# The next block's normed tokens: computed from the raw ones, turned by VectorE and HBM instead of TensorE

## The reference

```python
def rmsnorm(x, w, eps=EPS):
    return x * jax.lax.rsqrt(jnp.mean(x * x, axis=-1, keepdims=True) + eps) * w

def linear_attention(x, Wq, Wk, Wv, Wo, out_norm_w):
    # q, k, v = x @ Wq, x @ Wk, x @ Wv in 8 heads of 128, in chunks of 128 tokens
    def step(S, qkv):
        qb, kb, vb = qkv
        attn = jnp.einsum('bhid,bhjd->bhij', qb, kb)
        attn = jnp.where(causal, attn, 0.0)
        o = jnp.einsum('bhij,bhjv->bhiv', attn, vb) + jnp.einsum('bhid,bhdv->bhiv', qb, S)
        S = S + jnp.einsum('bhid,bhiv->bhdv', kb, vb)
        return (S, o)
    ...
    return rmsnorm(o, out_norm_w) @ Wo

xn = _layernorm(x, axis=-1)
h = rmsnorm(xn, attn_norm_w)
x1 = xn + linear_attention(h, Wq, Wk, Wv, Wo, attn_out_norm_w)
h = rmsnorm(x1, mlp_norm_w)
s = x1 + jax.nn.silu(h @ Wgate) * (h @ Wup) @ Wdown
g = _silu(ffn_fp4(xn, w_gate, w_up, w_down))
out = x + s * g
```

## Time and profile before

| | us |
|---|---|
| median of 3 runs | 1061.51 |
| lowest, highest | 1060.58, 1062.41 |
| the profiled execution | 1064.03 |
| its span | 1062.3 |

### The profile page before, as it was taken

The page is one execution under the profiler, slowest core; times in us unless marked ns, Lnnn a source line. Parts: engine busy times, 40 slices in busy tenths (PEclk is TensorE's granted clock), DMA queues, the critical chain, the costliest instruction groups (busy, mean ns, idle before and its releaser), DMA issues.

```text
span 1062.3 us, 18981 instructions
## 1 busy us (share of the span) xinstructions
PE 1051.6 (99%) x6790; PEld 960.8 (90%) x6790; DVE 891.8 (84%) x1860; ACT 558.5 (53%) x1604; POOL 47.3 (4%) x68
## 2 busy tenths in 40 slices
PE   9999999999999999999999999999999999999998
PEld 6899999989989999998999889999999999999997
DVE  6788888888877888888777898888888888888887
ACT  6765765756656657657565634443333333333332
POOL 1000000000000000000000000101001010101010
PEclk9999999999999999999999999999999999999999
DMA  6555355455363553654445622253323233323213
GB/s 218 163 171 168 109 173 169 137 157 167 135 191 115 173 179 120 188 171 128 162 149 185 175 73 91 81 159 100 115 90 120 85 120 99 120 85 96 83 59 112
DMA packets 166222, 143.10 MB, mean 135 GB/s; under 512 B 28784, under 2 KB 162928, under 8 KB 166128
## 3 DMA queue, kind: packets, MB, share of 16 engines
q1 hardware_dynamic: 165440, 141.88, 42.9%
q10 hardware_dynamic: 688, 0.00, 0.0%
HBM read 77.27 MB, written 64.57 MB: 134 GB/s over the span
## 4 chain that ended last, share of the span: by engine, by line
PE 88%; DMA 5%; DVE 3%; ACT 2%; SPq 1%; issue 1%; POOL 0%; DVEq 0%; ACTq 0%; POOLq 0%
PE ps L263 69%; PE ps L724 4%; PE ps L776 4%; PE ps L770 4%; PE ps L754 4%; DMA moved<-work 2%; DMA r_gate<-moved 2%; SPq L417 1%; PE ps L859 1%; PE ps L652 1%; PE ps L612 0%; DVE work L1404 0%; DVE work L1521 0%; ACT work L947 0%; ACT work L994 0%
## 5 line engine op out<-in xcount | busy, mean ns | idle before, releaser
L263 PE MATMUL ps<-r_k,r_gate_up 128*128 128x512 f32 x768 | 185.2, 391 | 0.7 <-DVE r_k L1587 0.7
L263 PEld LDWEIGHTS ps<-r_k,r_gate_up 128*128 128x128 f32 x768 | 141.5, 188 | 28.1 <-issue 0.9
L263 PE MATMUL ps<-r_o,onT 128*128 128x256 f32 x768 | 106.8, 288 | 0.0
L263 PE MATMUL ps<-r_h,r_k 128*128 128x512 f32 (+1 forms) x393 | 105.2, 403 | 0.0
L263 PEld LDWEIGHTS ps<-r_q,r_v 128*128 128x128 f32 x768 | 99.7, 191 | 4.9 <-DVE r_v L1655 0.3
L263 PE MATMUL ps<-r_q,r_v 128*128 128x256 f32 x768 | 102.3, 283 | 0.0
L967 ACT ACTIVATE work<-ps 128x128 f32<-128x128 f32 x256 | 67.3, 278 | 59.4 <-PE ps L776 59.1
L263 PE MATMUL ps<-r_h,r_q 128*128 128x512 f32 x384 | 98.2, 391 | 0.0
L263 PE MATMUL ps<-r_v,r_h 128*128 128x512 f32 x384 | 97.4, 390 | 0.0
L263 PEld LDWEIGHTS ps<-r_o,onT 128*128 128x128 f32 x768 | 95.8, 190 | 0.1
L1162 ACT ACTIVATE r_v<-work 128x512 fp32r<-128x512 f32 x64 | 40.5, 633 | 99.2 <-DVE work L1651 99.1
(11 more groups left out here) (161 smaller groups left out, 2054.2 us busy)
## 6 DMA issues: line engine op xcount, KB each, us to landing
moved<-work SPq DMA_DIRECT2D x63, 512.0 KB, 2.9
r_gate<-moved SPq DMA_DIRECT2D x252, 128.0 KB, 2.5
kept_h<-work SPq DMA_DIRECT2D x31, 384.0 KB, 2.6
work<-kept_h SPq DMA_DIRECT2D x124, 96.0 KB, 2.2
work<-in_L_attn_hidden_states SPq DMA_DIRECT2D x15, 512.0 KB, 5.3
kept<-work SPq DMA_DIRECT2D x9, 514.0 KB, 4.4
kept_h<-work SPq DMA_DIRECT2D x9, 512.0 KB, 3.4
kept_xq<-work SPq DMA_DIRECT2D x8, 512.0 KB, 5.6
```

What stands on the lines that cost most here:

```text
L263: done = pe.matmul(out_ap, a, b, start=first and n == 0, stop=last and n == 2, skip_group_check=skip)
```

## The change

`turn_h` leaves TensorE's program. `normed_h` no longer reads `xn` but `x_in`: VectorE makes two factors (`h_factors`, step h = 1), the product of the layer norm's and the rms factor and minus the mean times it, and ScalarE's `normed_h`, now at the end of step h = 1, applies them as scale and bias into `h_sb`. In step h = 2, after `normalize`, VectorE transposes `h_sb` in 32x32 blocks into `x_in`, which nobody needs any more. In step h = 3 SP stores `x_in` to a new HBM tensor `kept_h`, right behind the store of k and o, and loads it back into `h_flat` with its quarters in place, behind the loads of k and o. In step h = 4 ScalarE's `turned_hi` (after `copy_q` and `first_state`) and VectorE's `turned_lo` (first of the early extras, in eight pieces of 128 columns) make `hT`. TensorE's values of that step and their wait go to the step's end, behind the output projection, and ScalarE's copy of them to the end of its step. The piece's transpose into `h_flat` waits for `turned_lo`, `normed_h2` for the store of `x_in`.

```diff
+    kept_h = nc.dram_tensor("kept_h", (HALVES, QUADS, P, KD * CH * QUAD), F32).ap()
...
# SP, exchange (next_h = n + 1 in step h = CH - 1)
                     sp.dma_start(moved.rearrange("b p x -> p b x"), leaving.rearrange("p b i x -> p b (i x)"))\
                       .then_inc(moved_out, 16)
+                    if next_h is not None:
+                        sp.wait_ge(h_turned, KD + next_h)
+                        sp.dma_start(kept_h[next_h % HALVES].rearrange("a p x -> p a x"),
+                                     in_quads(x_in.rearrange("p c d -> p (c d)"))).then_inc(h_stored, 16)
...
+                    if next_h is not None:
+                        sp.wait_ge(h_stored, 16 * next_h)
+                        load_turned(h_flat, kept_h[next_h % HALVES], h_loaded)
...
# TensorE, score_and_project
-                    if h == CH and ahead:
-                        pe.wait_ge(hT_ready, (n0 + s) * KD + 2 * KD)
...
-                    if ahead or h < CH:
+                    if (ahead or h < CH) and h != CH:
                         values(*((1, h, s) if h < CH else (0, h - CH, 1 - s)))
# TensorE, attend
-                    if h == CH - 1 and ahead:
-                        pe.wait_ge(h_ready, n0 + s + 1)
-                        pe.wait_ge(k_perm_ready, t0 + j + 2)
-                        pe.wait_ge(k_ready, t0 + j + 2)
-                        turn_h(0)
-                        pe.wait_ge(attn_ready, t0 + j + 1)
-                        turn_h(1)
...
+                    if h == CH and ahead:
+                        pe.wait_ge(hT_ready, (n0 + s) * KD + 2 * KD)
+                        values(0, 0, 1 - s)
# ScalarE
+                def normed_h(n):
+
+                    act.wait_ge(h_factor_ready, n)
+                    act.wait_ge(gu_ready, n + 1)
                     for c in range(CH):
-                        done = act.activation(h_sb[:, c, :], xn[:, parity, c, :], ACT.Copy, scale=small[:, HR, c:c + 1])
+                        done = act.activation(h_sb[:, c, :], x_in[:, c, :], ACT.Identity, bias=small[:, HB, c:c + 1],
+                                              scale=small[:, HG, c:c + 1])
...
+                def turned_hi(parity, n):
+                    act.wait_ge(h_loaded, 16 * QUADS * n)
+                    for k in range(KD):
+                        act.activation(as_tokens(hT[:, parity, HI, k, :]), landed(h_flat, k), ACT.Copy,
+                                       scale=nw_attn[:, k:k + 1]).then_inc(hT_hi, 1)
...
-                        act.wait_ge(xn_ready, min(value + 1, BLOCKS))
+                        act.wait_ge(h_stored, 16 * min(value, BLOCKS - 1))
...
-                    if h == CH - 1 and ahead:
-                        turned_hi(0, 1 - s, (n0 + s) * KD + KD + 1)
-                        turned_hi(1, 1 - s, (n0 + s) * KD + KD + 2)
+                    if h == CH and ahead:
+                        turned_hi(1 - s, n0 + s + 1)
...
+                    if h == CH and ahead:
+                        copy_v(t0 + j + CH + 1, 0, 0)
...
-                    if h == 2 and ahead:
-                        normed_h(1 - s, n0 + s + 2)
+                    if h == 1 and ahead:
+                        normed_h(n0 + s + 1)
# VectorE
+                def h_factors(parity, mine):
+
+                    settled(dve.tensor_tensor(small[:, HG, :], small[:, HR, :], ln_factor[:, parity, 0, :], ALU.mult), mine)
+                    dve.scalar_tensor_tensor(small[:, HB, :], mv[:, parity, :, 0], -1.0, small[:, HG, :],
+                                             ALU.mult, ALU.mult).then_inc(h_factor_ready, 1)
...
+                def turned_lo(parity, n):
+                    for k in range(KD):
+                        dve.wait_ge(hT_hi, n * KD + k + 1)
+                        for c in range(CH):
+                            done = dve.scalar_tensor_tensor(as_tokens(hT[:, parity, LO, k, :])[:, c],
+                                                            landed(h_flat, k)[:, c], nw_attn[:, k:k + 1],
+                                                            as_tokens(hT[:, parity, HI, k, :])[:, c].bitcast(F32),
+                                                            ALU.mult, ALU.subtract)
+                        done.then_inc(hT_ready, 1)
# early_extras
+                    if h == CH and ahead:
+                        turned_lo(1 - s, n + 1)
                     if h == CH and rounds_piece:
+                        dve.wait_ge(hT_ready, (n + 2) * KD)
                         dve.transpose(h_flat[:, 0:PIECE4[n - 1]].rearrange("p (b t) -> p b t", t=QUAD),
# late_extras
                     if h == 2 and ahead:
                         normalize(1 - s)
-                    if h == CH - 1 and ahead:
-                        turned_lo(0, 1 - s, n * KD + KD + 1)
-                        turned_lo(1, 1 - s, n * KD + KD + 2)
+                        dve.wait_ge(xn_ready, n + 2)
+                        dve.wait_ge(h_ready, n + 1)
+                        turn_blocks(x_in.rearrange("p c d -> p (c d)"), h_flat, h_turned)
# attention, after rms_factor in h == 1
+                        h_factors(1 - s, mine)
```

## The result

The changed kernel takes 1114.87 us (median of 4, 1113.4 to 1115.33) against 1061.12 for the kernel before (median of 4): a ratio of 1.050, with an interval of 1.0486 to 1.0512. The forecast was slower, 1091.5, in a range to 1110; the time lies above it. Its profiled execution took 1114.95 us, span 1113.2.

What follows compares the result with a forecast made beforehand. The prediction took TensorE, busy 99% at full clock, to bound the kernel. Its terms, -6.1 + 2.0 + 0.2 + 3.1 + 31.8 - 0.9, made +30.1: 1094.1 us profiled, 1091.5 in the median, range 1076 to 1110.

Steps and rivals of the forecast that it cites:

- What bounds it, and the sign: Attention part: TensorE bounds the kernel; after the change its fifth steps wait for VectorE's additions; slower, chance 0.92.
- Transposes, -6.1: Fourth steps: removing TensorE's eight transposes saves 0.88 us in each of seven, all on the path, -6.1 us.
- Second step, +2.0: Second steps: two 4-element VectorE operations ahead of turned k cost 0.28 us each, +2.0 us in all.
- Third step, +0.2: Third steps: the earlier normed_h delays k's copy and exchange, but TensorE has values and q meanwhile, +0.2 us in all.
- Fourth step, 3.1 given back of 6.1: Fourth steps: VectorE's block transposes make additions late, losing 0.7 us in four odd blocks, about 0.1 in three even, +3.1.
- Fifth step, +31.8: Fifth steps: TensorE waits for additions behind VectorE's turned_lo, itself waiting for ScalarE; +31.8 us over seven blocks.
- 10.9 + 1.48 + 1.37: Fifth step: additions end at 10.9, then 1.48 to the next scores and 1.37 for values: 13.75 us against 8.92.
- TensorE's clock falls in the gap: Rival: the fifth step's idle gap brings half clock, 3 us lost each; 1101, or 1112 in all blocks; chance 0.18.
- Queues: SP's added store and four loads: the tile lands 0.9 to 1.4 us before ScalarE needs it in the fifth step; no cost.
- the tile lands late: Rival: the tile lands 1.5 us after ScalarE is ready in every block's fifth step, +10, 1101; chance 0.12.
- covered after all: Rival: in the fifth step TensorE does not wait for VectorE's additions; only small terms stay, 1056.7 to 1059.8; chance 0.06.
- HI halves come early: Rival: without VectorE's wait for ScalarE, fifth steps cost only 2.4 us each, 17 in place of 31.8, 1076.7; chance 0.12.

Runs made afterwards that it cites:

- e3: Kernel before with each of the eight TensorE transposes in the fourth step done twice; 1070.15 us against 1062.46, ratio 1.0075.
- e4: Kernel before with only h_factors and the early normed_h (scale and bias, from x_in) added, transposes still on TensorE; 1065.34 us against 1062.46, ratio 1.003.
- e5: e4 plus VectorE's two block transposes at the end of the third step, result unread; 1065.33 us against 1061.62 for the kernel before, ratio 1.0036.
- e2: Changed kernel with the fifth step's turned_lo and piece transpose moved behind VectorE's state additions, weights4_hi behind ScalarE's normed o; 1073.41 us, ratio 1.0113 to the kernel before.
- e1: Changed kernel with 20 extra, later overwritten products filling TensorE's gap in each fifth step; 1100.12 us, ratio 1.0358 to the kernel before.
- e6: e2 with h_factors moved to the second step's late extras and ScalarE's last copy of values ahead of weights4_hi; 1072.09 us, ratio 1.0093 to the kernel before.
- e8: Changed kernel with 10 extra products instead of the 20 of e1 in each fifth step's gap; 1109.56 us, ratio 1.044 to the kernel before.

## Why the prediction was wrong

**What bounds it, and the sign:** right. A VectorE addition behind an early extra, named by L770, in seven steps.

**Transposes, -6.1:** right in six blocks (e3: 0.87 to 0.88 a step). In the first it was not "all on the path": twice the transposes cost only 0.2 there.

**Second step, +2.0:** right in kind and size (0.23 to 0.38 each in six blocks; the second block's, 0.6 late in the kernel before for another reason, came out 0.39 shorter). **Third step, +0.2:** mis-sized, +2.3. The prediction took for granted that values and q would hide it. ScalarE's timeline of the kernel before has the older form, without a bias, a step later:

```profile
194.38 1.70 ACT L925 ACTIVATE work<-work 128x256 f32<-128x256 f32 x4
```

With a bias it is 2.08, and k's copy waits behind it (e4); on average 0.33 a step comes through. **Fourth step, 3.1 given back of 6.1:** the lost part was 4.1. Three odd blocks lost 0.63 each (forecast 0.7), three even ones 0.31 to 0.38 (0.1), for the reason put (e5); the first block's step came out 0.39 longer than before, 1.3 lost, which the prediction had counted with the odd ones. VectorE's block transposes are what costs there (0.41 in e5, with TensorE's still in place).

**Fifth step, +31.8:** the structure came out to a tenth: L754's new place at 3.66, the idle time 3.39 to 5.67 of VectorE (forecast 3.35 to 5.7), 6.1 without the early extra (e2; forecast 6.07). The step that failed is the last of its sum, "10.9 + 1.48 + 1.37". The 10.9 was 11.5, from the eight pieces: 2.19 where 1.6 was taken between bounds of 1.3 and 2.5; such a piece from SBUF takes 0.345 and starts 0.263 after the one before, where 0.20 was taken. Over the seven steps the additions end 3.8 later than forecast. The larger part is the 1.48 + 1.37: durations at full clock, read from a trace without a gap. From the last addition to the next scores the seven steps took 34.0 in place of 7 x 2.85 = 20.0; that is 14.0, and e1 gives 12.8 of them back, the third block's to 2.87. The other 1.2 are mostly the even blocks, where 3.21 follow the last addition even at full clock. This was the rival "TensorE's clock falls in the gap", in its place, at a lower price than put (3 us each forecast, 12.7 / 7 = 1.8 measured), but it was set beside the central case when it follows from it: the forecast itself had TensorE stand for 4.7 us, and nothing in the trace of before, whose longest idle time of TensorE's products in the attention part is 0.7, showed that it keeps full speed behind such a gap. The clock fell in all seven gaps of 4.1 to 5.2 us. There the trace agrees with the rule of the Trainium skill ("TensorE: Matmul & The Clock Gate", Part 1) that stood beside that rival. With the gap filled (e1, 1100.1) the time lies inside the forecast's range. That the rival's 1112 for all seven blocks lies so near to 1114.87 is partly luck: the clock's share is 12.7 and not 21, and the pieces (3.8), the third step (2.1), the fourth (1.0) and what follows make up for it.

**The rest.** The spans differ by 50.9, forecast 30.1: 20.8 more. The fifth step has 16.9 of them, the third and fourth 3.1, the others 0.8. In the medians it is 2.6 more still, since the prediction took off 2.5 for the profiled execution of the kernel before, and that of the changed kernel lies at its median (1114.95 and 1114.87). The seventh step of the last block is 3.4 longer: SP issues the store of k at 624.52 and the loads at 630.11, 5.6 later instead of 3 (two other stores of 512 KB stand 2.0 ahead of it, 2.9 in the kernel before), TensorE idles 2.5 and the clock falls there too (636.1 to 639.5).

```profile
622.01 0.43 SPq L451 DMA_DIRECT2D kept<-work  x1
622.48 0.43 SPq L460 DMA_DIRECT2D kept_xq<-work  x1
624.52 0.36 SPq L412 DMA_DIRECT2D moved<-work  x1
630.11 1.75 SPq L424 DMA_DIRECT2D r_gate<-moved  x4
```

e3 and e6 have 1.4 and 1.5 there, the other six nothing (three of them 1.1 to 1.7 in the step before it). Against it stands a late exchange in the fifth block's first step of the kernel before (1.7), which six of the eight experiments lack too. Whether such late exchanges have a cause in the change wasn't settled.

**Queues:** "the tile lands 0.9 to 1.4 before ScalarE gets to it" was too early by half a microsecond: in the changed kernel the last load is issued 0.3 to 1.7 after the fifth step's start and lands 3.5 to 4.4 after it. It cost nothing, since ScalarE came at 4.5 to 4.9; the rival "the tile lands late" is out, with less to spare than thought.

**The other side** ("covered after all") would have needed the additions by 6.07; they came at 10.6 to 11.6. **"HI halves come early"** is out as well: VectorE waited 1.8 to 2.3 for them in every block.

## What to carry to other kernels

Where engines work in program order, an operation that waits must not stand ahead of one that the critical engine needs: the same work, moved behind the additions, cost 41 us less (1114.9 to 1073.4), the clock's share in it included. When a forecast puts an idle gap of several microseconds into a TensorE that had none, price the work behind the gap at the lower clock too; durations from the gapless trace don't hold there. And work taken from the bounding engine is worth its time only as far as the others were not hidden behind it: of 0.88 in the fourth step 0.25 to 0.57 came back in the blocks behind the first.

## What the runs showed of the hardware

TensorE's granted clock fell to 0.50, its lower level of 1.2 GHz, in seven of seven gaps of 4.1 to 5.2 us. It fell 2.4 to 4.8 us into the gap, while the engine stood idle, and was back at 1.00 only 3.3 to 5.6 us after work had begun again (223.1, with the work from 224.74, and 229.9 in the block above). Around idle times of 1.8 to 3.1 it fell in five of seven, and there 0.2 to 1.6 us after TensorE had resumed (e8). Feeding the idle engine products that nobody needs was a net gain of 14.8 us in the medians (e1).

A three-operand VectorE instruction on 128x128 from SBUF took 0.345 us, and such instructions started 0.263 apart: four of them are done in 1.13. The kernel before does the same work in one on 128x512 with its input in PSUM, in 0.74 (L1298). No run has the uncut one from SBUF, so how much of the difference the cutting costs isn't shown.
